# One-hots and low row numbers by quarters, x0 in two signals, coefficient matmuls in two runs

## What is computed

```python
e = jnp.stack([tbl_0[ids[:, 0]], ..., tbl_15[ids[:, 15]]], axis=1)
A  = jnp.repeat(x0, 16, axis=1)                    # b, n = 624, h
Bm = jnp.repeat(e, 39, axis=2).reshape(b, 624, 16)
z  = jnp.einsum('bnh,bnd,nk,khd,kd->bkh', A, Bm, alpha, w, hv[..., 0])
h = jnp.concatenate([z.reshape(b, -1), dense_ctx], axis=1)
h = jnp.maximum(h @ W_top1 + b_top1, 0.0)
h = jnp.maximum(h @ W_top2 + b_top2, 0.0)
y = h @ W_top3
```

## Time and profile before

| | us |
|---|---|
| median of 3 runs (198.88, 200.86, 201.39) | 200.86 |
| the profiled execution, its own time | 200.86 |
| its span, first to last instruction | 199.1 |
| TensorE matmuls busy | 166.9 (84%) |
| VectorE busy | 148.7 (75%) |
| GpSimd busy | 112.8 (57%) |
| ScalarE busy | 65.3 (33%) |

### The profile page before, as it was taken

The page is one execution under the profiler, slowest core; times in us unless marked ns, Lnnn a source line. Parts: engine busy times, 40 slices in busy tenths (PEclk is TensorE's granted clock), DMA queues, the critical chain, the costliest instruction groups (busy, mean ns, idle before and its releaser), DMA issues.

```text
span 199.1 us, 5053 instructions
## 1 busy us (share of the span) xinstructions
PE 166.9 (84%) x2170; PEld 123.9 (62%) x2170; DVE 148.7 (75%) x171; ACT 65.3 (33%) x203; POOL 112.8 (57%) x119
## 2 busy tenths in 40 slices
PE   0427994837969999999689999998999899899983
PEld 0427894814745776778457767685776567467661
DVE  3698999189769798998999958759977893794000
ACT  2692019400241183136011731360128118211312
POOL 2887778777777777777777777777771000000000
PEclk9999998585978999999999999999999999999999
DMA  5687779999999917930089269300990980000000
GB/s 122 189 288 199 193 177 213 216 261 201 235 349 226 203 30 176 201 69 7 10 194 211 38 160 212 74 10 10 237 193 11 229 196 2 3 0 0 3 0 2
DMA packets 11698, 26.63 MB, mean 134 GB/s; under 512 B 3836, under 2 KB 6396, under 8 KB 9628
## 3 DMA queue, kind: packets, MB, share of 16 engines
q1 hardware_dynamic: 7756, 25.22, 53.5%
q0 software_dynamic: 3632, 1.06, 4.5%
q10 hardware_dynamic: 288, 0.04, 0.1%
HBM read 26.26 MB, written 0.05 MB: 132 GB/s over the span
## 4 chain that ended last, share of the span: by engine, by line
PE 51%; POOL 15%; DVE 13%; issue 9%; DMA 7%; ACT 3%; DVEq 0%; POOLq 0%
POOL e_all L335 15%; PE bank L678 14%; PE bank L699 13%; PE bank L709 12%; DVE prod L579 10%; PE bank L629 6%; DMA e_all<-tbl,ids_sb 5%; PE bank L668 3%; PE bank L693 3%; ACT spread L406 2%; DMA ids_sb<-ids 2%; DVE picked L538 2%; DVE onehot L526 1%; PE bank L718 1%; ACT h_sb L424 0%
## 5 line engine op out<-in xcount | busy, mean ns | idle before, releaser
L335 POOL DMA_INDIRECT e_all<-tbl,ids_sb x112 | 111.4, 994 | 36.0 <-issue 33.8
L579 DVE TENSOR_TENSOR prod<-x_main,bank 128x2048 f32<-128x2048 f32 x32 | 72.2, 2280 | 14.1 <-issue 8.8
L678 PE MATMUL bank<-prod,coef 128*32 128x256 f32 x640 | 44.2, 397 | 9.5 <-DVE prod L579 9.5
L629 PE MATMUL bank<-parts,onehot 125*128 125x80 bf16 (+1 forms) x864 | 38.7, 210 | 4.5 <-DVE onehot L526 4.3
L629 PEld LDWEIGHTS bank<-parts,onehot 125*128 125x128 bf16 x864 | 36.5, 107 | 8.3 <-DVE parts L504 3.5
L406 ACT ACTIVATE spread<-e_all 128x128 f32<-128x128 f32 (+3 forms) x128 | 29.0, 329 | 16.8 <-DMA e_all<-tbl,ids_sb 16.7
L678 PEld LDWEIGHTS bank<-prod,coef 128*32 128x32 f32 x640 | 17.2, 111 | 24.3 <-DVE prod L579 13.2
L699 PE MATMUL bank<-z_sb,w1z_sb 128*128 128x256 f32 x128 | 30.3, 380 | 0.0
L709 PE MATMUL bank<-h_sb,w_sb 128*128 128x256 f32 x128 | 29.8, 386 | 0.7 <-ACT h_sb L416 0.7
L709 PEld LDWEIGHTS bank<-h_sb,w_sb 128*128 128x128 f32 x128 | 23.7, 190 | 6.9 <-ACT h_sb L416 3.1
L416 ACT ACTIVATE h_sb<-bank 128x512 f32<-128x512 f32 x16 | 9.6, 597 | 53.3 <-PE bank L699 53.3
(11 more groups left out here) (41 smaller groups left out, 63.6 us busy)
## 6 DMA issues: line engine op xcount, KB each, us to landing
x_main<-x_m SPq DMA_DIRECT2D x16, 512.0 KB
x_last<-x_l SPq DMA_DIRECT2D x8, 1024.0 KB
low_h<-low_dram SPq DMA_DIRECT2D x6, 768.0 KB, 14.2
e_all<-tbl,ids_sb POOLq DMA_INDIRECT x112
x_last<-dense_t SPq DMA_DIRECT2D x8, 128.0 KB
prod<-small_tables SPq DMA_DIRECT2D x1, 672.0 KB, 5.4
w1z_sb<-w1z SPq DMA_DIRECT2D x1, 512.0 KB, 13.3
w_sb<-w SPq DMA_DIRECT2D x1, 512.0 KB, 13.7
```

Source lines behind the costliest of these rows:

```text
L335: pool.indirect_dma_start(out=e_all[:, t * E + s * D:t * E + (s + 1) * D], out_offset=None, in_=tables[s], in_offset=bass.IndirectOffsetOn ...
L579: dve.tensor_tensor(prod[:, c, :, :], x0[:, p, :, :], value_bank(g, c // 2)[:, c % 2 * GB:(c % 2 + 1) * GB].unsqueeze(1).broadcast_to([P, ...
L629: last = pe.matmul(look_ps[i % 2][:, t * w:(t + 1) * w], onehot[:, n, c, at:at + P], parts[:, part, col:col + w], start=(t == 0 and c == 0 ...
L678: last = pe.matmul(z_ps[p][32 * q:32 * q + 32, a * GB:(a + 1) * GB], coef[:, c, 4 * a + q, :], prod[:, c, 4 * a + q, :], start=(c == 0 and ...
```

## The change

`QUARTER` is 512. `onehot` holds one quarter, and `low_h` two quarters in two buffers, each with semaphores of its own. `make_onehot` works on 512 columns and is called for every unit: 36 calls with two instructions each, instead of 18. `load_low(u)` loads one quarter in three DMAs; quarter 0 is loaded where half 0 was, quarter 1 behind x0 of group 0, quarters 2 and 3 ahead of the main tiles of groups 2 and 4. The semaphore `x0_in` becomes `main_in` and `last_in`; VectorE waits for main before step 0 and for last before step 4. The main tile of group g is asked for once product 3 of group g-2 is made, its last tile once product 4 is. Main(1) goes out before the dense layers' weights, last(1) after them. On TensorE all 16 `main_coef` run before the look-ups and the `last_coef` in fours behind look-ups 2, 4, 6 and 8.

```diff
-COEF_FROM = 3
+LAST_COEF_AT = (2, 4, 6, 8)
...
-        onehot = sb("onehot", [RC, NSMALL, 2, HALF], BF16)
+        onehot = sb("onehot", [RC, NSMALL, 2, QUARTER], BF16)
-        low_h = sb("low_h", [P, NSMALL, HALF], F16)
+        low_h = sb("low_h", [P, 2, NSMALL, QUARTER], F16)
...
-            def load_low(a, n, count):
+            def load_low(u):
+                if u >= 2:
+                    sp.wait_ge(onehot_ready, 2 * NSMALL * (u - 1))
+                for n in range(0, NSMALL, 3):
+                    sp.dma_start(low_h[:, u % 2, n:n + 3, :], low_dram[n:n + 3, u * QUARTER:(u + 1) * QUARTER].unsqueeze(0).broadcast_to(
+                        [P, 3, QUARTER])).then_inc(low_in[u % 2][n // 3], 16)
...
-            for n in range(0, NSMALL, 3):
-                load_low(0, n, 3)
+            load_low(0)
...
+            def load_main(g, p):
                 for j in range(2):
+                    sp.dma_start(x0_main[64 * j:64 * j + 2 * FM, p, :, :], x0_m[g]).then_inc(main_in[p], 16)
+            def load_last(g, p):
                 sp.dma_start(x0_last[:, p, :, :], x0_l[g].unsqueeze(1).broadcast_to(
+                    [2 * 8, J, HP * GB])).then_inc(last_in[p], 16)
...
-            load_x0(0, 0)
+            load_main(0, 0)
+            load_last(0, 0)
+            load_low(1)
+            load_main(1, 1)
...
-            load_x0(1, 1)
-            sp.wait_ge(onehot_ready, 2 * NSMALL)
-            for n in range(0, NSMALL, 3):
-                load_low(1, n, 3)
+            sp.wait_ge(dense_low, 4)
+            load_last(1, 1)
             for g in range(2, GROUPS):
-                load_x0(g, g % 2)
+                sp.wait_ge(product_ready, NC * (g - 2) + MC)
+                if g % 2 == 0 and g // 2 + 1 < 4:
+                    load_low(g // 2 + 1)
+                load_main(g, g % 2)
+                sp.wait_ge(product_ready, NC * (g - 1))
+                load_last(g, g % 2)
...
             for i in units_at(0):
-                if i // NSMALL % 2 == 0:
-                    make_onehot(i)
+                make_onehot(i)
...
-                dve.wait_ge(x0_in[p], 16 * X0_LOADS * (g // 2 + 1))
+                dve.wait_ge(main_in[p], 32 * (g // 2 + 1))
                 for c in range(NC):
+                    if c == MC:
+                        dve.wait_ge(last_in[p], 16 * (g // 2 + 1))
...
-                pe.wait_ge(onehot_ready, 2 * (u // 2 * NSMALL + n + 1))
+                pe.wait_ge(onehot_ready, 2 * (i + 1))
...
-            for k in range(K - NSMALL + 1):
+            for k in range(K):
                 main_coef(k)
...
-                if n > 0:
-                    main_coef(K - NSMALL + n)
-                if n == COEF_FROM:
+                if n in LAST_COEF_AT:
                     pe.wait_ge(blast_done, 1)
-                if n >= COEF_FROM:
-                    for k in range(made, made + 2):
+                    for k in range(made, made + K // len(LAST_COEF_AT)):
                         last_coef(k)
-                    made += 2
+                    made += K // len(LAST_COEF_AT)
```

More of the change, by code:

```diff
@@ L61 @@
 TILES = B // P
-HALF = B // 2
+HALF, QUARTER = B // 2, B // 4
 GB = 256
@@ L235, in dlrm_tower @@
         low_stored = sem("low_stored")
-        low_in = [sem(f"low_in{i}") for i in range(NSMALL // 3)]
+        low_in = [[sem(f"low_in{u}_{i}") for i in range(NSMALL // 3)] for u in range(2)]
         pick_ready = sem("pick_ready")
@@ L251, in dlrm_tower @@
         gathered = [sem(f"gathered{i}") for i in range(2)]
-        x0_in = [sem(f"x0_in{i}") for i in range(2)]
+        main_in = [sem(f"main_in{i}") for i in range(2)]
+        last_in = [sem(f"last_in{i}") for i in range(2)]
         spread_ready = sem("spread_ready")
@@ L264, in dlrm_tower @@
         stored = sem("stored")
-        PREP_LOADS, MLP_LOADS, X0_LOADS, DENSE_LOADS = 2, 4, 3, 12
+        PREP_LOADS, MLP_LOADS, DENSE_LOADS = 2, 4, 12
         block = ctx.enter_context(nc.Block())
@@ L277, in _ @@
             sp.dma_start(table_sb, small_tables).then_inc(table_in, 16)
-            def load_low(a, n, count):
-                sp.dma_start(low_h[:, n:n + count, :], low_dram[n:n + count, a * HALF:(a + 1) * HALF].unsqueeze(0).broadcast_to(
-                    [P, count, HALF])).then_inc(low_in[n // 3], 16)
-            sp.wait_ge(low_stored, 16)
-            for n in range(0, NSMALL, 3):
-                load_low(0, n, 3)
-            def load_x0(g, p):
-                if g >= 2:
-                    sp.wait_ge(product_ready, NC * (g - 1))
+            def load_low(u):
[4 more added lines that the diff above has]
+                        [P, 3, QUARTER])).then_inc(low_in[u % 2][n // 3], 16)
+            sp.wait_ge(low_stored, 16)
+            load_low(0)
+            def load_main(g, p):
                 for j in range(2):
-                    sp.dma_start(x0_main[64 * j:64 * j + 2 * FM, p, :, :], x0_m[g]).then_inc(x0_in[p], 16)
-                if g == 1:
-                    sp.wait_ge(dense_low, 4)
+                    sp.dma_start(x0_main[64 * j:64 * j + 2 * FM, p, :, :], x0_m[g]).then_inc(main_in[p], 16)
+            def load_last(g, p):
                 sp.dma_start(x0_last[:, p, :, :], x0_l[g].unsqueeze(1).broadcast_to(
-                    [2 * 8, J, HP * GB])).then_inc(x0_in[p], 16)
+                    [2 * 8, J, HP * GB])).then_inc(last_in[p], 16)
             for n in range(NSMALL // 3):
-                sp.wait_ge(low_in[n], 16)
+                sp.wait_ge(low_in[0][n], 16)
             for q in range(4):
@@ L519, in make_onehot @@
             def make_onehot(i):
-                n, a = i % NSMALL, i // (2 * NSMALL)
-                dve.wait_ge(low_in[n // 3], 16 * (a + 1))
-                if a > 0:
+                n, u = i % NSMALL, i // NSMALL
+                dve.wait_ge(low_in[u % 2][n // 3], 16 * (u // 2 + 1))
+                if u > 0:
                     dve.wait_ge(onehot_used, i - NSMALL + 1)
                 for c in range(2):
-                    dve.tensor_scalar(onehot[:, n, c, :], low_h[0:RC, n, :], low_sb[:, c:c + 1], None,
+                    dve.tensor_scalar(onehot[:, n, c, :], low_h[0:RC, u % 2, n, :], low_sb[:, c:c + 1], None,
                                       ALU.is_equal).then_inc(onehot_ready, 1)
```

4 lines of the change are left out of this document (1 added, 3 removed).

## The result

The changed kernel takes 206.28 us (median of 4 runs, 205.03 to 208.77), the kernel before 200.17 in the same comparison (4 runs, 198.88 to 201.39): ratio 1.027, 95% interval 1.016 to 1.038. It is slower, and above the range.

What follows compares the result with a forecast made beforehand. Before 60.7 us the SP queue and VectorE bound the kernel, afterwards TensorE. Terms -0.3 + 0.4 - 0.85 + 1.1 = +0.35, rounded to +0.5 on 200.86, gave 201.4 us; range 197.5 to 205.0.

Steps and rivals of the forecast that it cites:

- the rival with packets that cost the same at 1 KB: Start: 96 ns packets, first loads save nothing, first product +3.4, total 204.9 us; chance 0.16, shared with per-instruction cost.
- The pair of one-hots: VectorE, every unit: a 512-wide one-hot takes 0.27 us, 0.54 a pair, with 0.4 and 0.79 as ends.
- The coefficient matmuls: TensorE, head: moving main coefficients out of look-ups is worth about 1.9 us there, nothing by itself, as VectorE idles 5.34.
- Groups 4 and 5: New one-hot pairs of units 33 and 34 push products behind TensorE's waits at 138.21 and 141.32: 1.1 us lost.
- groups 2 and 3: Shorter one-hot pairs ahead of three products that TensorE waits for: 0.85 us gained.
- First loads: Head, SP queue: three low-number loads with half the bytes, same packets, save 2.9 us (ends nothing and 3.5).
- What is put behind it: Before the first product: a third of quarter 1 behind x0 adds 1.5 us (1.2 to 2.3), four one-hots 1.1.
- Group 0: VectorE: six one-hot pairs, 3.2 us, fill holes of 1.13 and 1.69 us as far as gathers allow; 0.4 left.
- x0 of later groups: Loads after group 0: x0's issue to landing, 14 us, fits into TensorE's 16 us of work; no gain, no loss.
- The gathers rival: Group 1: its last gather lands near 57 us, delaying its first product 3.8, in all 205.0 us; chance 0.15.

Runs made afterwards that it cites:

- the two like kernels: Changed kernel with quarter 3 loaded behind x0 of group 3: 203.92 us, ratio 1.021; changed kernel with coefficient matmuls woven into look-ups again: 205.64 us, ratio 1.031.
- two kernels above: Kernel before with only x0's main and last signals split: 199.52 us, ratio 1.003; changed kernel with quarter 1 between main and last of group 0's x0: median 203.76 us.

## Why the prediction was wrong

**Right.** The mechanism at the first product: quarter 1 stands behind both tiles of x0, VectorE's wait is ended by `low_h`, the separate signal of main buys nothing there, and the four one-hots cost 1.1 us. The first product of the rival with packets that cost the same at 1 KB was put at 44.1 and its time at 204.9; the profile has 44.60, the median is 206.28. That 44.60 comes so near is partly luck: 1.1 us of it are the later start of that execution, and the two like kernels have 41.8 and 41.9. The pair of one-hots, 0.54 taken, is 0.52. The coefficient matmuls are worth nothing, and no later product waits for x0. Groups 4 and 5: 1.1 forecast, 0.92 measured. In groups 2 and 3 the pairs gave 0.74 (look-up to contraction on TensorE: 5.55 after 5.78 us for the second product of group 2, 5.79 after 6.03 and 3.64 after 3.91 around 103 and 107) where 0.85 was forecast.

**The step that failed** is *First loads*: "I take 2.9 saved". The first loads saved nothing in the profiled pair, 10.55 us against 10.45, and some 0.8 over the other profiles. With the later start the dense loads went out at 20.77 instead of the forecast 16.7, and x0 of group 0 at 27.32 instead of 23.8; in the kernel with quarter 3 earlier it was 25.73. I had both ends, nothing and 3.5, and took nearly the upper one because a packet of half the size is busy half as long. That is true and beside the point: with half the bytes the engines were busy 55.2% instead of 82.4% of the stretch, and the packets came at 149 a microsecond instead of 138, so something other than the engines' time for the bytes set the pace. With 0.8 in place of 2.9 the forecast of 201.4 becomes 203.5; with the lower end of this term and the upper one of the next (*What is put behind it*) it is the rival's 204.9. Neither reaches 206.28; the stop below is missing from both. The term for the third of quarter 1, 1.5, was too small in the profile, where it took 16.20 us from the issue of x0 to the end of VectorE's wait against 14.05 before, 2.15 more, and too large in the two like kernels, with 14.89 and 14.96.

**A second size** was *Group 0*: "They fill the holes ... 0.4 is left". In the profiled pair it looks right, 0.71. But the size of the holes belongs to the execution: group 0 takes 20.04, 17.30 and 18.91 us in three executions of the kernel before, 17.03 with the coefficient matmuls alone and 20.55 with the one-hots, and the one-hots alone lose 3 us in all, where the terms for them add up to 1.75 (1.1 + 0.4 - 0.85 + 1.1). One profile can't tell a hole that is always there from one that was there that time; that the second hole went back to a DMA was a sign.

**Put at nothing without a reason** is the second loss, the stop in group 3. *x0 of later groups* ("No gain and no loss") asked only whether x0 comes in time, which it does. It did not ask what else uses the DMA engines: TensorE's own instructions. The stop cost 1.15 us of the profiled difference (17.28 against 16.13), and up to 4.45 in the kernels that have it; with 203.5 that makes 204.6 to 208, an estimate from these profiles. How much of the 206.28 is the start and how much the stop in a typical execution is not settled, since one profile is all there is of the changed kernel.

**The gathers rival** did not come about by the change: group 1's gathers ended at 49.98 in the profile after, earlier than before. The trace still shows them as what holds group 1 whenever the start is early (50.3 and 53.53 us in two kernels above). The Trainium skill's rule of turns between queues (its page "DMA: Bandwidth & Descriptors", section "Queues, rings and completion order") would have voided this rival. The late gathers of group 1 in the kernel with quarter 1 ahead of last, 53.53 us and a wait of 3.07 us on VectorE, go against using it so; no run here tests the turns themselves.

## What to carry to other kernels

When a load is cut into parts that are "fetched when needed", the place of each part in the queue is the change, more than its size: two parts moved gave back all of the 2.7%. Ask for each part what is ahead of it in its queue, who waits for it, and what else is about to use the DMA engines, instructions included. A signal split in two helps only if nothing new is put behind the first half, and its gain lasts only up to the next late input, here the gathers; it can still be worth its time where other work, here the one-hots, fills what it opens. And look at more than one execution before a hole is counted as cover.

## What the runs showed of the hardware

- A load that reads a row into many partitions, on an empty queue, takes 11.5 to 13.5 us for 1152 packets, whether of 512 bytes, 1 KB or 2 KB; from rows of their own 2.5, 5 and 8 us. In the head of this kernel such packets came at 138 a microsecond, 965 in 7 us, with 2 KB in each, and at 149, 1046 in 7 us, with 1 KB.
- TensorE stopped for 0.57 to 2.26 us, by the times for want of instructions, where their 16 KB block started 6 to 9 us later than in kernels without a load there. The profile gives such a stop as idle time ended by "issue", inside a run of like matmuls.
- After the stop of 2.26 us the granted clock of TensorE was 0.50 from 112 to 114 us, the lower level, and group 3 took 4.45 us more than in the kernel without the stop.
